# Three graph layers over 100,000 edges: a table of sources and segments, turned attributes in fours, and a program without a loop

## The reference, cut to what matters

```python
ew = edge_attr @ edge_w + edge_b
rel_masks = [(edge_type == i).astype(x.dtype) for i in range(NUM_REL)]
inv_cnt = [1.0 / jnp.maximum(jax.ops.segment_sum(m, dst, num_segments=n), 1.0) for m in rel_masks]
for l in range(N_LAYERS):
    residual = x
    msg = jax.nn.relu(x[src] * ew)
    out = jnp.zeros((n, D), dtype=x.dtype)
    for i in range(NUM_REL):
        h = jax.ops.segment_sum(msg * rel_masks[i][:, None], dst, num_segments=n)
        h = h * inv_cnt[i][:, None]
        out = out + h @ weights[l, i]
    out = out + x @ roots[l] + biases[l]
    x = residual + jax.nn.relu(out)
```

## Time and profile before

| | us |
|---|---|
| median of the timed runs | 6061.88 |
| the timed runs, lowest and highest | 6043.99, 6080.07 |
| profiled execution, first to last instruction (the only time that the profile gives of it) | 8152.7 |
| POOL busy, share of that span | 4095.4, 50% |
| PE busy, share | 5238.7, 64% |
| DVE busy, share | 4249.1, 52% |
| ACT busy, share | 2292.6, 28% |

### The profile page before, as it was taken

The page is one execution under the profiler, slowest core; times in us unless marked ns, Lnnn a source line. Parts: engine busy times, 40 slices in busy tenths (PEclk is TensorE's granted clock), DMA queues, the critical chain, the costliest instruction groups (busy, mean ns, idle before and its releaser), DMA issues.

```text
span 8152.7 us, 89562 instructions
## 1 busy us (share of the span) xinstructions
PE 5238.7 (64%) x25082; PEld 3212.9 (39%) x25082; DVE 4249.1 (52%) x9658; ACT 2292.6 (28%) x5880; POOL 4095.4 (50%) x4199
## 2 busy tenths in 40 slices
PE   5256666478777835666666665666666566666668
PEld 1133333255555523444434443333333334333345
DVE  6665555455555524355555554555555455555543
ACT  0034444344444411222222221222222122222221
POOL 2344444565665561255555545555555455555530
PEclk9577777677777757878777787878888777778779
DMA  3010000132322210333333333333333333333320
GB/s 111 15 30 17 17 17 16 39 82 80 84 79 78 79 36 20 94 100 98 100 99 99 100 91 96 104 100 104 102 106 104 86 99 101 99 99 102 98 68 16
DMA packets 445005, 624.93 MB, mean 77 GB/s; under 512 B 97099, under 2 KB 330261, under 8 KB 444564
## 3 DMA queue, kind: packets, MB, share of 16 engines
q0 software_dynamic: 187648, 457.52, 20.5%
q1 hardware_dynamic: 250164, 159.14, 6.8%
q10 hardware_dynamic: 6754, 2.96, 0.2%
HBM read 556.32 MB, written 62.94 MB: 76 GB/s over the span
## 4 chain that ended last, share of the span: by engine, by line
PE 28%; DVE 14%; another core or an unknown queue 10%; issue 9%; ACT 1%; DVEq 1%; DMA 0%; POOL 0%; SPq 0%; ACTq 0%; POOLq 0%
PE banks L1165 15%; DVE acc_mem L1683 6%; DVE z_mem L1826 5%; PE banks L1195 4%; PE banks L1153 3%; PE banks L1108 2%; PE banks L1098 2%; PE banks L1150 1%; ACT z_mem L801 1%; DVE z_mem L1814 1%; PE banks L1185 1%; DVEq L1683 1%; DVE z_mem L1843 0%; PE banks L1137 0%
## 5 line engine op out<-in xcount | busy, mean ns | idle before, releaser
L615 POOL DMA_INDIRECT sort_mem<-x_d,x_mem x2568 | 2459.2, 958 | 2298.3 <-issue 1164.0
L1165 PE MATMUL banks<-z_mem 128*128 128x257 f32 x5136 | 1885.1, 500 | 1597.7 <-DVE acc_mem L1683 1177.4
L1165 PEld LDWEIGHTS banks<-z_mem 128*128 128x128 f32 x5136 | 1060.9, 238 | 2383.3 <-issue 1175.8
L1683 DVE TENSOR_TENSOR acc_mem<-acc_mem,banks 128x257 f32 x2568 | 1083.4, 422 | 873.7 <-PE banks L1165 466.1
L1826 DVE TENSOR_TENSOR z_mem<-banks,sort_mem 128x512 f32<-128x512 f32 x1284 | 826.9, 686 | 1221.8 <-remote 677.7
L801 ACT ACTIVATE z_mem<-z_mem 128x512 f32<-128x512 f32 x1284 | 768.9, 628 | 1996.0 <-DVE z_mem L1826 1538.1
L573 POOL DMA_INDIRECT recB_d<-acc_mem,sort_mem x740 | 745.6, 1008 | 892.8 <-DVE sort_mem L1415 676.5
L582 POOL DMA_INDIRECT acc_mem<-h_d,xnt_mem x808 | 824.5, 1020 | 552.3 <-PE banks L1041 332.4
L1041 PE MATMUL banks<-acc_mem,xnt_mem 128*128 128x257 f32 x1616 | 683.0, 542 | 377.0 <-DVE acc_mem L1626 217.9
L999 PE MATMUL banks<-xnt_mem,acc_mem 125*128 125x512 f16 (+1 forms) x3200 | 672.1, 375 | 355.9 <-ACT acc_mem L674 267.3
L999 PEld LDWEIGHTS banks<-xnt_mem,acc_mem 125*128 125x128 f16 x3200 | 340.9, 108 | 664.5 <-DVE xnt_mem L1528 329.8
(11 more groups left out here) (344 smaller groups left out, 5596.1 us busy)
## 6 DMA issues: line engine op xcount, KB each, us to landing
x_mem<-recB_d SPq DMA_DIRECT2D x642, 68.0 KB
sort_mem<-x_d,x_mem POOLq DMA_INDIRECT x2568
x_mem<-at_d SPq DMA_DIRECT2D x428, 64.0 KB
at_d<-x_mem SPq DMA_DIRECT2D x214, 64.0 KB
acc_mem<-h_d,xnt_mem POOLq DMA_INDIRECT x808
x_mem<-x_d SPq DMA_DIRECT2D x100, 128.0 KB
acc_mem<-in_edge_attr SPq DMA_DIRECT2D x40, 312.5 KB
recB_d<-acc_mem,sort_mem POOLq DMA_INDIRECT x740
```

Source lines behind the costliest of these rows:

```text
L615: pool.indirect_dma_start(out=xg[h % XG][:, k, :], out_offset=None, in_=x_ds[l % 2], in_offset=bass.IndirectOffsetOnAxis(ap=reci[h][:, k, ...
L1165: m.matmul(bank[5 + tile % 2][:, :AC], oneh[:, Q % 2, k, :], msg[:, Q % 2, k, :], start=True, stop=True)\
L1683: v.tensor_tensor(a_, a_, bank_[:, :AC], ALU.add).then_inc(flushed, 1)
```

## The change

Layer one keeps its record loads. While a quad's record is in its buffer, ACT now also copies its four sources and four segments into a small buffer (`keep_index`, two activations of 128x4). Every eight quads SP stores that buffer to DRAM (`store_index`, 27 stores). After layer one SP loads the whole table, 856 pairs for each partition, into the place of the record buffers (`load_table`, one transfer). In layers two and three there are no record loads: POOL takes the gathers' row numbers and DVE the segments from the table.

The turned attributes are loaded four quads at a time in layers two and three (`load_at`), into one half of the 8 buffers while PE uses the other.

POOL's program of layers two and three is written out, 1712 gathers, with a wait for `multiplied` ahead of each fourth. In layer one it stays a loop. The buffer x2w moves to make room, `attr_packed` is now named `rec_read`, and `fed_before` and `kept_before` go.

```diff
+        def fours_before(l, h):
+
+            return 16 * turns(4 * h) + (l - 1) * 16 * ((FOURS + 1 - h) // 2)
...
+        tab_mem = x_mem[:, 16 * D:16 * D + 2 * TB]
+        tab, tabi = ((tab_mem if dt == FP32 else tab_mem.bitcast(dt)).rearrange("p (t w) -> p t w", w=2) for dt in (FP32, INT32))
+        kept_mem = z(4104, 2 * 64).rearrange("p (g n) -> p g n", g=2)
...
-            def feed(l, Q):
+            def feed(Q):
 
                 h = Q % TURN
                 if Q >= TURN:
-                    if l == 0:
-                        sp.wait_ge(S("attr_packed"), Q - TURN + 1)
+                    sp.wait_ge(S("rec_read"), Q - TURN + 1)
                     x_ = (Q - TURN) % XG
...
+            def store_index(Q):
+
+                g, n = Q // TURN, Q % TURN + 1
+                sp.wait_ge(S("rec_read"), Q + 1)
+                if g:
+                    sp.wait_ge(S("table_moved"), 16 * g)
+                sp.dma_start(tab_d[:, 64 * g:64 * g + 8 * n], kept_mem[:, g % 2, :8 * n]).then_inc(S("table_moved"), 16)
+
+            def load_table():
+
+                sp.wait_ge(S("rec_read"), QB)
+                for x_ in range(XG):
+                    sp.wait_ge(S(f"landed{x_}"), landed_before(1, x_))
+                sp.wait_ge(S("seg_ready"), QB)
+                sp.wait_ge(S("table_moved"), 16 * EIGHTS)
+                sp.dma_start(tab_mem, tab_d).then_inc(S("table_moved"), 16)
...
-            def load_at(l, Q):
-
-                h = Q % TURN
-                if Q < TURN:
-                    sp.wait_ge(S(f"at_moved{h}"), kept_before(l, h))
-                sp.wait_ge(S("projected"), l * QB + max(0, Q - TURN + 1))
-                sp.dma_start(at[:, h, :], at_d[:, Q * P:(Q + 1) * P]).then_inc(S(f"at_moved{h}"), 16)
+            def load_at(l, f):
+
+                n = min(4, QB - 4 * f)
+                if l == 1 and f < 2:
+                    for h in range(TURN):
+                        sp.wait_ge(S(f"at_moved{h}"), 16 * turns(h))
+                sp.wait_ge(S("projected"), l * QB + max(0, 4 * f - 4))
+                sp.dma_start(at[:, f % 2 * 4:f % 2 * 4 + n, :].rearrange("p h n -> p (h n)"),
+                             at_d[:, 4 * f * P:(4 * f + n) * P]).then_inc(S(f"at_moved{f % 2 * 4}"), 16)
...
                 for Q in range(TURN, QB + lag):
-                    if Q < QB:
-                        feed(l, Q)
                     if l == 0:
+                        if Q < QB:
+                            feed(Q)
                         store_at(Q - lag)
-                    else:
-                        load_at(l, Q)
+                        if (Q - lag) % TURN == TURN - 1 or Q - lag == QB - 1:
+                            store_index(Q - lag)
+                    elif Q % 4 == 0:
+                        load_at(l, Q // 4)
...
                 if l < LAYERS - 1:
-                    for Q in range(TURN):
-                        feed(l + 1, Q)
-                        load_at(l + 1, Q)
+                    if l == 0:
+                        load_table()
+                    for f in range(2):
+                        load_at(l + 1, f)
...
-                looped(pool, TB // 4 // TURN, gather_x)
-                gather_x(TB // 4 // TURN, TB // 4 % TURN)
+                if l == 0:
+                    looped(pool, TB // 4 // TURN, gather_x)
+                    gather_x(TB // 4 // TURN, TB // 4 % TURN)
+                    continue
+
+                if l == 1:
+                    pool.wait_ge(S("table_moved"), 16 * EIGHTS + 16)
+                for Q in range(QB):
+                    pool.wait_ge(S("multiplied"), l * 2 * QB + max(0, 2 * Q - 2 * XG + 2))
+                    for k in range(4):
+                        pool.indirect_dma_start(
+                            out=xg[Q % XG][:, k, :], out_offset=None, in_=x_ds[l % 2],
+                            in_offset=bass.IndirectOffsetOnAxis(ap=tabi[:, 4 * Q + k, 0:1], axis=0))\
+                            .then_inc(S(f"landed{Q % XG}"), 16)
...
+                def keep_index(Q, h):
+
+                    g = Q // TURN
+                    if g >= 2 and h == 0:
+                        act.wait_ge(S("table_moved"), 16 * (g - 1))
+                    act.wait_ge(S(f"fed{h}"), g * 16 + 16)
+                    a.activation(kepti[:, g % 2, 4 * h:4 * h + 4, 0], reci[h][:, :, W_SRC], ACT.Copy)
+                    a.activation(kept[:, g % 2, 4 * h:4 * h + 4, 1], rec[h][:, :, W_SEG], ACT.Copy)
...
                     if l == 0 and Q + 5 < QB:
+                        keep_index(Q + 5, (Q + 5) % TURN)
                         pack_attr(Q + 5, (Q + 5) % TURN, (Q + 5) // TURN)
...
-                        pe.wait_ge(S(f"at_moved{h}"), kept_before(l, h) + Q // TURN * 16 + 16)
+                        pe.wait_ge(S(f"at_moved{Q // 4 % 2 * 4}"), fours_before(l, Q // 4 % 2) + Q // 8 * 16 + 16)
...
-                    dve.wait_ge(S(f"fed{h}"), fed_before(l, h) + Q // TURN * 16 + 16)
+                    if l == 0:
+                        dve.wait_ge(S(f"fed{h}"), Q // TURN * 16 + 16)
+                    else:
+                        dve.wait_ge(S("table_moved"), 16 * EIGHTS + 16)
+                    segments = tab[:, 4 * Q:4 * Q + 4, 1:2] if l else rec[h][:, :, W_SEG:W_SEG + 1]
```

More of the change, by code:

```diff
@@ L47 @@
 SCATTERED_FIRST = RANKED_FIRST + PAIRS // 4
-assert TB // 4 % TURN == 6
+assert TB // 4 % TURN == 6 and TURN == 8
+FOURS, EIGHTS = -(-(TB // 4) // 4), -(-(TB // 4) // 8)
 assert TA % 8 == 0 and PAIRS % 4 == 0
@@ L270, in build @@
                      for dt in (FP32, INT32))
+        tab_mem = x_mem[:, 16 * D:16 * D + 2 * TB]
+        tab, tabi = ((tab_mem if dt == FP32 else tab_mem.bitcast(dt)).rearrange("p (t w) -> p t w", w=2) for dt in (FP32, INT32))
+        kept_mem = z(4104, 2 * 64).rearrange("p (g n) -> p g n", g=2)
+        kept, kepti = ((kept_mem if dt == FP32 else kept_mem.bitcast(dt)).rearrange("p g (t w) -> p g t w", w=2)
+                       for dt in (FP32, INT32))
         at = x_mem[:, 0:TURN * P].rearrange("p (h n) -> p h n", h=TURN)
@@ L302, in build @@
         at_d = dram("at_d", [P, QB * P])
+        tab_d = dram("tab_d", [P, 2 * TB])
         x2_d = dram("x2_d", [NP_, D])
@@ L400, in _ @@
             recs = recB_d[0:P * TB, :].rearrange("(p t) w -> p (t w)", p=P)
-            def feed(l, Q):
+            def feed(Q):
                 h = Q % TURN
                 if Q >= TURN:
-                    if l == 0:
-                        sp.wait_ge(S("attr_packed"), Q - TURN + 1)
+                    sp.wait_ge(S("rec_read"), Q - TURN + 1)
                     x_ = (Q - TURN) % XG
[L408 to L414, removed]
+                    sp.wait_ge(S(f"landed{x_}"), landed_before(0, x_) + (Q - TURN) // XG * 64 + 64)
+                    sp.wait_ge(S("seg_ready"), Q - TURN + 1)
                 sp.dma_start(rec[h].rearrange("p k w -> p (k w)"),
                              recs[:, Q * 4 * RW:(Q + 1) * 4 * RW]).then_inc(S(f"fed{h}"), 16)
+            def store_index(Q):
[11 more added lines that the diff above has]
+                sp.dma_start(tab_mem, tab_d).then_inc(S("table_moved"), 16)
             def store_at(Q):
@@ L608, in gather_x @@
                         Q = TURN * i + h
-                        pool.wait_ge(S(f"fed{h}"), fed_before(l, h) + i * 16 + 16)
+                        pool.wait_ge(S(f"fed{h}"), i * 16 + 16)
                         if due(2 * Q - 2 * XG + 2):
-                            pool.wait_ge(S("multiplied"), l * 2 * QB + 2 * Q - 2 * XG + 2)
+                            pool.wait_ge(S("multiplied"), 2 * Q - 2 * XG + 2)
                         pool.sem_inc(S("passed_pool"), 1)
@@ L789, in pack_attr @@
                 def pack_attr(Q, h, n):
-                    act.wait_ge(S(f"fed{h}"), fed_before(l, h) + n * 16 + 16)
+                    act.wait_ge(S(f"fed{h}"), n * 16 + 16)
                     if due(Q - 1):
@@ L825, in _ @@
                     for q in range(5):
+                        keep_index(q, q)
                         pack_attr(q, q, 0)
@@ L1812, in compare @@
                     h = Q % TURN
-                    dve.wait_ge(S(f"fed{h}"), fed_before(l, h) + Q // TURN * 16 + 16)
+                    if l == 0:
[3 more added lines that the diff above has]
+                    segments = tab[:, 4 * Q:4 * Q + 4, 1:2] if l else rec[h][:, :, W_SEG:W_SEG + 1]
                     v.tensor_tensor(oneh[:, Q % 2, :, :], column_numbers.rearrange("p (a s) -> p a s", a=1).broadcast_to([P, 4, P]),
-                                    rec[h][:, :, W_SEG:W_SEG + 1].broadcast_to([P, 4, P]), ALU.is_equal)\
+                                    segments.broadcast_to([P, 4, P]), ALU.is_equal)\
                         .then_inc(S("seg_ready"), 1)
```

14 lines of the change are left out of this document (5 added, 9 removed).

## The result

The changed kernel takes 6103.02 us (median of four runs, 6078.54 to 6112.57). The kernel before took 6062.16 us beside it. The ratio is 1.0056 with an interval of 1.0033 to 1.0080, so it is slower by 20 to 49 us (the two medians alone would give 1.0067). The forecast was 6055. Among the timed runs of the kernel before in the experiments two took 6946.8 and 16163.7 us, with granted clocks of 0.63 and 0.52; the ratios leave them out, and the 8152.7 us of the profiled execution (clock 0.77) may be of their kind, which no run shows.

The account below looks back on a forecast made before the run. POOL's issue of gathers was taken to bound all three layers, about 1130 us each. The terms 0 + 0 - 5 + 0 + 5 summed to 0; the forecast was 6055, a few us under the median shown, range 5950 to 6105.

Parts of the forecast that it names:

- the term for layer one: ACT in layer one: two more activations a quad add 0.22 us each quad, 0 to 47 us, taken as +5.
- the second rival: Layer one's ACT loop becomes the bound, each quad over 5.0 us paying 0.22; up to +47, so 6105; chance 0.17.
- the stops: Stretches without DMA activity in the profiled execution; POOL stands 1054.3 us over three layers; taken as mostly lacking when timed.
- POOL's pace: POOL's gathers start 1.25 us apart, 5.0 us a quad, 1072 us a layer; said to bound all three layers.
- Record loads and transfers in fours worth 0: Layers two and three: dropping 428 record loads and loading turned attributes four quads a transfer, each valued at 0.
- POOL's program written out, -5: POOL, layers two and three: removing 428 waits and about 54 loop turns gains 5 us, from a range of -50 to 0.
- No stall on fetching it: POOL's written out program: waits over 1 us on "issue" every 256 instructions would have shown the forecast wrong.
- The table's load and its 27 stores hidden: Stores in layer one cost 0; the 877 KB load is covered by 21 us, 0, or +6 if it queued.
- The first rival: DMA relief is real time: packets saved count in timed runs too, in full -350, a time of 5710; chance 0.25.
- What I expected of the profile, 7800 us: Profiled span falls by about 350, to 7800, as the stops shrink with traffic, with no such gain in timed runs.

Follow-up runs that it names:

- the pair moved ahead: Changed kernel with the pair of small ACT activations placed behind the relu and ahead of the copy of turned attributes; 6041.3 us, ratio 1.0006 to the kernel before.
- POOL written out: Kernel before with only POOL's program of layers two and three written out in place of the loop; 6042.5 us, ratio 0.9998.
- the pair alone: Kernel before plus only the two small activations a quad on ACT in layer one, their output read by nobody; 6072.5 us, ratio 1.0056.
- the later copy: Either kernel with ACT copying turned attributes of quad Q+3 instead of Q+4 in layer one; kernel before 5988.1 us (0.9916), changed kernel 5989.6 us (0.9921).
- two pairs: Kernel before plus four small activations a quad on ACT in layer one, in place of the change's two; 6123.9 us, ratio 1.0137.

## Why the prediction was wrong

**The step that failed.** It is the term for layer one: "I take +5, because most quads have more slack than this one", out of a range of 0 to 47, with "four buffers let slow and quick quads even out". The mechanism was named, as the second rival, with place and price (6105); I gave it 0.17. The size was wrong: alone, the pair cost 30 us of layer one and 1.0042 to 1.0070 in the timed runs, 25 to 42 us. The duration was right: the pair adds 0.20 us to a turn of ACT's loop, where I had 0.22. A turn of the loop in the kernel before, from multiply to multiply:

```profile
2789.96 1.28 DVE L1826 TENSOR_TENSOR z_mem<-banks,sort_mem 128x512 f32<-128x512 f32 x2
...
2792.99 0.27 PE L1137 MATMUL banks<-ident,z_mem 128*128 128x128 f32 x1
...
2793.30 0.28 ACT L787 ACTIVATE x_mem<-banks 128x128 f32<-128x128 f32 x1 [2.77 <-PE banks L1137]
...
2793.47 0.30 ACT L794 ACTIVATE z_mem<-x_mem 128x128 f32<-128x128 f32 x1
...
2794.25 1.28 DVE L1826 TENSOR_TENSOR z_mem<-banks,sort_mem 128x512 f32<-128x512 f32 x2
```

And in the changed kernel:

```profile
2809.10 1.28 DVE L1872 TENSOR_TENSOR z_mem<-banks,sort_mem 128x512 f32<-128x512 f32 x2
...
2812.32 0.27 PE L1179 MATMUL banks<-ident,z_mem 128*128 128x128 f32 x1
...
2812.63 0.28 ACT L818 ACTIVATE x_mem<-banks 128x128 f32<-128x128 f32 x1 [2.77 <-PE banks L1179]
...
2812.80 0.20 ACT L834 ACTIVATE z_mem<-x_mem 128x4 int32<-128x4 int32 x1
2812.90 0.20 ACT L835 ACTIVATE z_mem<-x_mem 128x4 f32<-128x4 f32 x1
...
2813.00 0.30 ACT L825 ACTIVATE z_mem<-x_mem 128x128 f32<-128x128 f32 x1
...
2813.58 1.28 DVE L1872 TENSOR_TENSOR z_mem<-banks,sort_mem 128x512 f32<-128x512 f32 x2
```

4.29 us became 4.48. The packing starts 0.17 us after the copy in the one and 0.37 us in the other, and everything behind it on ACT, the next relu in the end, starts as much later. Both turns are under 5.0 us, as I argued.

What failed is that the buffers even this out. POOL can be at most four quads ahead, and the long steps come twice in a window of 8 or 9 quads. From its last gather of a quad to the first of the next POOL was held longer than 0.3 us at 26 quads of layer one in the kernel before, 31 us beyond the 0.3 in all, and at 49 quads, 66 us, in the changed kernel; in layer two of both at none. One of the long steps, from multiply to multiply at full clock, is 8.07 us in the kernel before and 8.26 in the changed one, where layer two has 7.2. The other is longer by more than the pair. In it ACT's three scaling copies (`flatten`) stand ahead of the relu as well, so that PE waits for that relu, and PE turns the window's sums. The row of one such step, and PE's sums in it, in the kernel before:

```profile
2657.55:2663.31 5.76, 3.48 (x25) 2.21 (x25) 3.57 (x9) 2.99 (x8) 4.24 (x6) 1.00 0.47 138
...
2658.89 1.11 PE L1165 MATMUL banks<-z_mem 128*128 128x257 f32 x4 [1.67 <-ACT z_mem L801]
...
2660.77 1.17 PE L1165 MATMUL banks<-z_mem 128*128 128x257 f32 x4 [0.77 <-DVE acc_mem L1683]
```

And at the same quad of the changed kernel, with a row for the part at the lower clock:

```profile
2675.73:2683.14 7.41, 4.91 (x25) 3.31 (x25) 3.58 (x9) 3.64 (x11) 5.58 (x7) 0.77 0.50 139
2679.20:2682.00 2.80, 2.80 (x9) 2.19 (x9) 1.42 (x4) 0.55 (x4) 2.04 (x3) 0.50 0.42 117
...
2677.27 1.11 PE L1207 MATMUL banks<-z_mem 128*128 128x257 f32 x4 [1.87 <-ACT z_mem L841]
...
2679.15 2.05 PE L1207 MATMUL banks<-z_mem 128*128 128x257 f32 x4 [0.77 <-DVE acc_mem L1725]
```

PE does the same 25 instructions in 5.76 and in 7.41 us. It waits 0.2 us longer for the relu (1.87 and 1.67), and then its granted clock stands at 0.50, the lower of its two levels, 1.2 in place of 2.4 GHz, and four matmuls take 2.05 us in place of 1.17. Over 23 of the 25 windows, all but the last two, this step met the lower level in 11 in the kernel before, in 9 with the pair moved ahead and in 11 with POOL written out; in 21 in the changed kernel, 19 with the pair alone and 21 with two; and in none with the later copy, of either kernel. Before the change it took 5.8 us at the full clock and 7.2 where it met the lower one, and in the changed kernel 6.0 and 7.8. In the mean it grew from 6.46 to 7.67 us; 23 x 1.21 is 28 us, an estimate, and about the whole loss of the layer. (The other long step met the lower level less often, in 3 windows in place of 11, and gives a little back: 8.72 us in the mean, then 8.47. With two pairs the step is 8.15 us, which is about half of the 77 us.) So the greater part of the loss isn't 0.2 us paid quad by quad. It is one step in each window that more often runs at the lower clock. That the longer wait of PE brings the clock down is argued from these counts; no run changes the one without the other.

The rival had both pieces, the windows' work and PE's lower clock, but took the clock as given and priced the pair at its own length in every quad. That its 6105 lies so near the measured 6103 is therefore in part luck. Its condition, a loop that "averages more than 4.8 us" without the stops, can't be settled by the mean step of layer one (5.36 us before and 5.49 after), because a mean step isn't shorter than POOL's pace: it is 5.03 in layer two, where only POOL is the bound. The condition itself was taken from one quad of 4.77 us, and a mean says little where two steps of a window hold POOL up.

**What could have told it.** With the stops in the trace POOL's slack could not be read off directly. The order on ACT I had read: the relu stands behind a copy that waits for PE's turn, which stands behind the sums of the same quad. What I didn't draw from it is that in such a ring any instruction counts in full at each quad in which the ring is the bound. Layer one was also 55 us longer than layer two in the long execution, 1527 us where the earlier trace rows has 1472, which the prediction doesn't take up:

```profile
3377.00:4904.00 1527.00, 998.75 (x5106) 618.14 (x5106) 785.55 (x1599) 401.82 (x1013) 831.88 (x857) 0.78 0.36 100
```

I had put all three layers at about 1130 us. In the kernel before they took 1174, 1100 and 1070.

**The other steps.** POOL's pace bounds layers two and three: right, 4 x 1.25 us, and nothing longer than 0.3 us between gathers in either kernel. It was said of all three layers, and in layer one it doesn't hold. Record loads and transfers in fours worth 0 in the timed runs: right; layers two and three of both kernels are equal to 4 us, and the two kernels with the later copy are equal within their intervals. (The "640 KB transfer" is a slip: four quads are 256 KB, which is what the estimate behind it uses.) POOL's program written out, -5 of a range of -50 to 0: measured 0.9998, with an interval of -10 to +8 us, in which -5 can't be told from nothing. No stall on fetching it: right, none longer than 0.3 us. The table's load and its 27 stores hidden: right, as the moved pair shows, since everything else of the change is in that kernel and it stands at 1.0006. The stops as something that the one profiled execution had and the timed ones lack: right; the same program profiled again has a span of 6038.6 us in place of 8152.7. The first rival, that relief of the DMA engines is real time, had 0.25 and is refuted: 23% of all packets less moved nothing, in the kernel with the pair moved ahead (0.9993 to 1.0020). What I expected of the profile, 7800 us, rested on the stops being a constant property of profiling; they are not, and what brings them on stays open.

The sum with the term as measured in the profiles is 0 + 0 + 0 + 0 + 28 less 4 in the window of layer two, 24 us, against 20 to 49 measured. The profiled executions also differ by 15 us ahead of the first gather of layer one (2405.6 and 2420.8). That stretch is the same code in both, and in the eight profiles it lies between 2405.6 and 2428.6 without following the edits, so I leave it as scatter (the long profile is left out of these eight).

## What to carry to other kernels

An engine at 38% busy can hold the critical ring: ask not how busy it is but what it waits for, and put new work ahead of that wait, not behind it. The same two instructions cost 0.6% behind ACT's wait and nothing in front of it. And a small addition to a ring can cost more than its own length where it lengthens a wait of PE: look at the granted clock of the longest steps, not only at the mean. Removing traffic gained nothing here, where the issue of gathers at 1.25 us each bounds the two layers that lost the traffic. And before idle time in a trace is priced, hold the profiled execution's own length against the timed runs; if they differ, profile the unchanged kernel again.

## What the runs showed of the hardware

One profiled execution of a program had 221 stretches of over 3 us without any DMA activity in its three layers, POOL waiting 1054 us on DVE in them, and PE's granted clock at 0.77. Another of the same program had five, 65 us of such waits, and a clock of 0.91. A step of 25 PE instructions took 5.76 us at the full clock and 7.41 us where 2.80 us of it were granted 0.50; PE had waited 1.67 and 1.87 us for a relu ahead of it. Small activations of 128x4 elements take 0.20 us each but start 0.10 us apart, so a pair adds 0.20 us to a chain. A written out program of 1712 indirect transfers on POOL, with 1.25 us a transfer, never waited for its instructions: the longest gap that isn't a change of layer is 0.3 us. In the changed kernel the gathers took 969 ns in the mean in layer one and 947 in layers two and three.
